# Product of gate and up kept in PSUM, unpaced sends, and earlier or split loads in an eight-layer hybrid kernel

## The reference

```python
x = x + attn_a(layernorm(x))        # layer 0, 16 heads of 8
x = x + experts(layernorm(x))       # layer 1
x = x + attn_b(layernorm(x))        # layer 2, 32 heads of 32
x = x + experts(layernorm(x))       # layer 3
x = x + attn_pos(layernorm(x))      # layer 4, bias from a FIR filter table
x = x + int8_ffn(layernorm(x))      # layer 5
x = x + linear_attention(layernorm(x))   # layer 6
x = x + int8_ffn(layernorm(x))      # layer 7

def experts(x):                     # 7 routed experts, top 2, DFF = 512
    out = swiglu(x, shared_gate, shared_up, shared_down)
    probs = softmax(x @ router_w.T)
    top_vals, top_idx = top_k(probs, 2)
    top_vals = top_vals / (top_vals.sum(-1) + 1e-9)
    for e in range(7):
        out += combine[:, e] * swiglu(x, gate[e], up[e], down[e])
    return out                      # swiglu: (silu(x @ gate.T) * (x @ up.T)) @ down.T
```

## Time and profile before

| what | value |
|---|---|
| time, median of three runs | 4055.63 us |
| profiled execution: its own time | 4050.18 us |
| profiled execution: span of the trace | 4048.4 us |
| PE busy (matmul) | 3387.4 us, 84% |
| DVE busy | 3025.4 us, 75% |
| ACT busy | 2472.5 us, 61% |
| POOL busy | 1173.4 us, 29% |
| layers 1 and 3 (experts) | about 812 to 1223 us and 2511 to 2923 us of the span |
| layers 5, 6, 7 | about 3551 to 3622, 3628 to 3961, 3968 to 4040 us |

### The profile page before, as it was taken

One profiled execution on the slowest core, in us unless ns is written; L12 is line 12 of the kernel. 1 busy time (PEld: TensorE's weight loads), 2 busy tenths in 40 slices (PEclk: granted clock), 3 DMA queues, 4 the chain that ended last, 5 costly groups with the idle time before them and its releaser, 6 DMA issues. The chain is left out here.

```text
span 4048.4 us, 57724 instructions
## 1 busy us (share of the span) xinstructions
PE 3387.4 (84%) x18344; PEld 2100.8 (52%) x18344; DVE 3025.4 (75%) x7013; ACT 2472.5 (61%) x4541; POOL 1173.4 (29%) x920
## 2 busy tenths in 40 slices
PE   5888888677964999999999997879499999858875
PEld 3555555465742455555455554657366666533433
DVE  6999999665874677777776773668778888659985
ACT  3888888534741556556555563457279999752325
POOL 1000000034431556665665664434300000010111
PEclk9999999878986999999999997889799999978887
DMA  4222221112435666767676660134332222200000
GB/s 130 46 53 53 46 37 24 29 49 91 145 106 86 87 88 85 89 83 89 82 90 84 88 87 9 51 113 140 100 106 47 46 30 47 34 26 0 0 0 27
DMA packets 218722, 265.93 MB, mean 66 GB/s; under 512 B 95745, under 2 KB 123714, under 8 KB 218295
## 3 DMA queue, kind: packets, MB, share of 16 engines
q1 hardware_dynamic: 208694, 241.25, 33.8%
q0 software_dynamic: 9728, 20.99, 1.5%
HBM read 103.36 MB, written 57.08 MB: 40 GB/s over the span
## 5 line engine op out<-in xcount | busy, mean ns | idle before, releaser
L1157 DVE TENSOR_REDUCE at_b_top<-ps 128x1 f32<-128x512 f32 x1024 | 662.5, 682 | 354.8 <-PE ps L917 353.5
L1046 ACT ACTIVATE at_b_e<-ps 128x512 f32<-128x512 f32 x1024 | 583.4, 598 | 474.7 <-PE ps L923 461.4
L585 ACT ACTIVATE at_a_e<-at_a_logits,at_a_neg_top 128x512 f32<-128x512 f32 x1024 | 655.9, 715 | 122.0 <-DVE at_a_neg_top L645 120.4
L816 POOL TENSOR_TENSOR at_b_e_pair<-at_b_e 128x1024 f32<-128x1024 f32 x256 | 603.1, 2376 | 403.1 <-PE ps L945 400.8
L505 PE MATMUL ps<-at_a_in_k,at_a_in_q 96*128 96x512 f32 x1024 | 477.9, 492 | 143.2 <-DVE at_a_clipped L613 116.9
L917 PE MATMUL ps<-at_b_k,at_b_q 96*128 96x512 f32 x1024 | 500.0, 492 | 41.0 <-DMA at_b_k<-at_b_k_hi 38.6
L923 PE MATMUL ps<-at_b_q,at_b_k 98*128 98x512 f32 x1024 | 426.9, 418 | 19.7 <-ACT at_b_e L1046 19.2
L641 DVE CUSTOM_DVE_ANT_0 at_a_logits<-ps,at_a_in_strip 128x512 f32<-128x512 f32 x512 | 340.7, 689 | 84.3 <-PE ps L505 33.7
L505 PEld LDWEIGHTS ps<-at_a_in_k,at_a_in_q 96*128 96x128 f32 x1024 | 185.0, 190 | 355.6 <-DVE at_a_clipped L613 206.6
L613 DVE TENSOR_SCALAR at_a_clipped<-ps 128x512 f32<-128x512 f32 x512 | 352.6, 689 | 21.3 <-PE ps L505 20.2
L635 DVE CUSTOM_DVE_ANT_0 at_a_logits<-at_a_clipped,at_a_in_decay_strip 128x512 f32<-128x512 f32 x512 | 347.6, 684 | 0.0
(11 more groups left out here) (334 smaller groups left out, 6451.4 us busy)
## 6 DMA issues: line engine op xcount, KB each, us to landing
moe_stage<-in_moe_w SPq DMA_DIRECT2D x46, 768.0 KB, 4.3
at_b_q<-at_b_q_hi SPq DMA_DIRECT2D x128, 256.0 KB, 5.4
at_b_k<-at_b_k_hi SPq DMA_DIRECT2D x128, 256.0 KB, 7.4
at_b_q<-at_b_q_lo SPq DMA_DIRECT2D x64, 256.0 KB, 7.6
at_b_k<-at_b_k_lo SPq DMA_DIRECT2D x64, 256.0 KB, 7.9
slot_rows<-empty_slots SPq DMA_DIRECT2D x44, 288.0 KB, 4.8
moe_xg<-slot_rows SPq DMA_DIRECT2D x44, 288.0 KB, 4.6
at_a_in_q<-q_hi SPq DMA_DIRECT2D x128, 64.0 KB
```

The source lines that it names most:

```text
L585: act.activation(e[:, j, qb, :], logits[:, j % 2, qb, :], ACT.Exp, bias=neg_top[:, j % 2, qb:qb + 1]).then_inc(exp_done, 1)
L816: pool.tensor_tensor(e_pair[:, j, :, :], e[r][:, j, 0:2, :], e[r][:, j, 2:4, :], ALU.add).then_inc(pair_done, 1)
L1046: act.activation(e[r][:, j, b, :], g.ps[:, ST_BANK + b % 2, :], ACT.Exp).then_inc(exp_done, 1)
L1157: dve.tensor_reduce(top[:, t, j, qb:qb + 1], g.ps[:, bank, :], AX_X, ALU.max).then_inc(max_done, 1)
```

## The change

It has four parts. None changes what is computed.

1. **h stays in PSUM.** The buffer `h` is gone. DVE writes `gate * up` back over the up bank (`h_bank`), and `high_h` and `low_h` read it there. The bank may be overwritten only when `low_h` has read it, so `gate_up(m)` now waits for `h_lo_done` of step m - 2 where it waited for `h_done` of step m - 2.
2. **Sends and row weights.** The waits that paced the sends are removed. The weights `c1`, `c2` are computed earlier (before the counts arrive from PE) and travel with the sent rows, in one more column of `xs`. A routed unit's rows are multiplied by their weight when they leave PSUM: four instructions of 128x128 (`tensor_scalar`) in place of one copy of 128x512. At the end of a turn PE adds the two rows of a token in PSUM with two identity matmuls for each batch, and DVE adds the sum to `x_all` with one instruction of 128x512. Rows are numbered so that a partition's rows lie together in DRAM, and the loads go round three buffers.
3. **Constants and weights.** The 13 loads of the linear attention's constants are issued in layer 5, POOL sets their zeros and ones there, and the buffers stay allocated through layer 6. The converted weights `w` of layer 5 are kept for layer 7, which no longer loads and converts them.
4. **The table in two pieces.** `table` is loaded as rows 0 to 95 and rows 96 to 100, ahead of `taps` and `wp`.

```diff
@@ begin, SP
                     if b == 1:
-                        for dst, src in ((taps, a["taps"]), (table, a["line_table"]), (wp, a["wpos"])):
+                        for rows in (slice(0, 96), slice(96, 101)):
+                            sp.dma_start(table[rows], a["line_table"][rows]).then_inc(table_loaded, 16)
+                        for dst, src in ((taps, a["taps"]), (wp, a["wpos"])):
                             sp.dma_start(dst[:], src).then_inc(table_loaded, 16)
...
+class LinearConstants:
...
+    def zero(self, pool):
+        pool.memset(self.from_m[:], 0.0).then_inc(self.zeroed, 1)
+        pool.memset(self.one_row[:], 1.0).then_inc(self.zeroed, 1)
+
+    def load(self, sp):
...
+            sp.dma_start(dst, src).then_inc(self.loaded, 16)
...
@@ linear_attention: SP's list of loads and DVE's memsets removed
@@ integer_swiglu, SP / ACT / POOL / DVE
-                sp.dma_start(stage[:], packed[0]).then_inc(w_loaded, 16)
+                if first:
+                    sp.dma_start(stage[:], packed[0]).then_inc(w_loaded, 16)
+                    ahead.load(sp)
+                    sp.wait_ge(ahead.loaded, 16 * ahead.LOADS)
...
-                act.wait_ge(w_float, 1)
-                act.activation(w[:], stage_f[:], ACT.Copy).then_inc(w_done, 1)
+                if first:
+                    act.wait_ge(w_float, 1)
+                    act.activation(w[:], stage_f[:], ACT.Copy).then_inc(w_done, 1)
...
+                if first:
+                    ahead.zero(pool)
...
@@ dispatch_experts, SP
-                for b in range(B):
-
-                    wait(sp, added, TB * (b - 1))
+                for b in range(1, B + 1):
+
+                    wait(sp, summed, b - Y_RING)
                     for k in range(2):
...
+                        rows = g.y_slots[k * B * S:(k + 1) * B * S, :].rearrange("(p t) d -> p t d", t=T)
+                        sp.dma_start(pair(b, k).rearrange("p (t d) -> p t d", t=TB), rows[:, (b - 1) * TB:b * TB, :]
+                                     ).then_inc(y_loaded[(b - 1) % Y_RING], 16)
@@ POOL
                 def send(k, half):
                     for t in range(half * HALF, (half + 1) * HALF):
-
-                        unit, place = divmod(k * T + t, SENT_PER_UNIT)
-                        if place == 0 and unit < B:
-                            pool.wait_ge(gate_done, nth(unit + 1, 0))
-                        elif place == 0 and unit == B:
-                            pool.wait_ge(h_lo_done, C * B)
                         pool.indirect_dma_start(slots, bass.IndirectOffsetOnAxis(ap=pos[k][:, t:t + 1], axis=0),
                                                 xs[:, t, :], None).then_inc(sent[2 * k + half], 16)
 
+                pool.wait_ge(c_done, 2)
                 pool.wait_ge(pos_done, 1)
@@ PE
                     wait(pe, gate_done, m - 2)
-                    wait(pe, h_done, m - 2)
+                    wait(pe, h_lo_done, m - 2)
...
+                pe.wait_ge(h_done, C * UNITS)
+                for b in range(1, B + 1):
+                    pe.wait_ge(y_loaded[(b - 1) % Y_RING], 32 * ((b - 1) // Y_RING + 1))
+
+                    wait(pe, added, b - 2)
+                    for k in range(2):
+                        ins = pe.matmul(g.ps[:, G_BANK + b % 2, :], g.ident[:], pair(b, k), start=(k == 0), stop=(k == 1))
+                    ins.then_inc(summed, 1)
@@ ACT and DVE
-                    act.activation(h_hi[:, (m - 1) % C, :], h[:, m % 2, :], ACT.Copy).then_inc(h_hi_done, 1)
+                    act.activation(h_hi[:, (m - 1) % C, :], h_bank(m), ACT.Copy).then_inc(h_hi_done, 1)
...
-                    dve.tensor_tensor(h_lo[:, (m - 1) % C, :], h[:, m % 2, :], h_hi[:, (m - 1) % C, :].bitcast(F32),
+                    dve.tensor_tensor(h_lo[:, (m - 1) % C, :], h_bank(m), h_hi[:, (m - 1) % C, :].bitcast(F32),
                                       ALU.subtract).then_inc(h_lo_done, 1)
...
-                        dve.tensor_copy(y_tok[u % 2][:], y).then_inc(out_taken, 1)
+                        dve.wait_ge(share_done, slot_of(u) + 1)
+                        for s in range(TB):
+                            ins = dve.tensor_scalar(y_tok[u % 2][:, s, :], y[:, s, :],
+                                                    share[:, slot_of(u) % 4, s:s + 1], None, ALU.mult)
+                            ins.then_inc(out_taken if s == TB - 1 else y_scaled, 1)
...
-                                dve.tensor_tensor(h[:, m % 2, :], gate[:, m % 2, :], g.ps[:, U_BANK + m % 2, :], ALU.mult
-                                                  ).then_inc(h_done, 1)
+                                dve.tensor_tensor(h_bank(m), gate[:, m % 2, :], h_bank(m), ALU.mult).then_inc(h_done, 1)
...
-                            dve.scalar_tensor_tensor(g.x_all[:, t, :], stage[:, (b - 1) % 2, tb * DM:(tb + 1) * DM],
-                                                     c1[:, t:t + 1], g.x_all[:, t, :], ALU.mult, ALU.add
-                                                     ).then_inc(first_added, 1)
...
+                        x = batch_of(g.x_all, b)
+                        dve.tensor_tensor(x, g.ps[:, G_BANK + b % 2, :].rearrange("p (t d) -> p t d", t=TB), x, ALU.add
+                                          ).then_inc(added, 1)
```

More of the change, by code:

```diff
@@ L1787, in integer_swiglu @@
     with Phase(nc, name) as ph:
-        stage = ph.sb("stage", [P, W], I32)
-        stage_f = ph.sb("stage_f", [P, W])
-        w = ph.sb("w", [P, W], F32R)
+        first = ahead is not None
+        stage = ph.sb("stage", [P, W], I32) if first else None
+        stage_f = ph.sb("stage_f", [P, W]) if first else None
         shift = ph.sb("shift", [P, TILES])
@@ L1870, in _ @@
                         pe.wait_ge(x_lo_done, s - 1)
-                        if s - 1 == 1:
+                        if first and s - 1 == 1:
                             pe.wait_ge(w_done, 1)
@@ L2044, in w_load, with pair @@
             return 0 if u <= B else slot_of(u) + 1
+        def pair(b, k=None):
+            both_rows = stage[:].rearrange("p a w -> p (a w)")[:, (b - 1) % Y_RING * 2 * S:((b - 1) % Y_RING + 1) * 2 * S]
+            return both_rows if k is None else both_rows[:, k * S:(k + 1) * S]
         def w_part(part):
```

144 lines of the change are left out of this document (71 added, 73 removed).

## The result

The changed kernel took **4403.93 us** (median of four runs, 4400.92 to 4407.03), the kernel before beside it 4055.14 us: ratio 1.086, 95% interval 1.0841 to 1.0879, 349 us slower. The forecast had the direction and the largest term, but with 4265 us it is 139 us short, and 4404 lies outside its range. The same kernel measured a second time (run e16, on chip 0; which chip the first measurement used is not recorded) took **4277.00 us** (4276.51 to 4277.61; before beside it 4048.62 us; ratio 1.0565, interval 1.0547 to 1.0582). Nearly the whole miss of 139 us is the difference of 127 us between these two measurements. I call their profiles "after, first" (span 4402.5 us) and "after, second" (4274.9 us).

A forecast was written before the change was run, and what follows sets the result against it. PE was taken to bound the routed units (busy 209.65 of 215 us). Terms 296 - 44 - 15 - 16 - 8 - 3 = +210 on the profiled 4050.18 gave 4260, 5 us under the median, so 4265 us; range 4215 to 4380.

The forecast's parts named there:

- h in PSUM: Expert layers' steps: gate_up's wait for h_lo closes a chain, 3.65 us a step, +296 us for both turns.
- rival 1: Expert units: PE's clock falls in the chain's pauses; 4.95 us a step, 4567 us at half clock; chance 0.10.
- Rival 2: Expert units: the chain doesn't close, steps keep 2.38 us; 3969 us; chance 0.06.
- Sends without a pace: Gap before the routed units: sends stay hidden, PE waits only for DVE's last output; -22 us a turn, -44.
- the cover is ample: Sends: 64 take 82 us, ending near 942, with shared units ending near 975, so even slower sends stay hidden.
- The bound from above: Sends without a pace: nothing is lost if POOL is slower, down to 1.8 us a send.
- Start: Kernel's start: split table spreads over the DMA engines, last batch at 12.5; -16 us, bounds 0 and -18.
- End of a turn: First load to last statistics: 21.3 us in place of 28.8; -15 for both turns, bounds +11 and -20.
- Layers 6 and 7: ACT starts layer 6 earlier, -8 us; layer 7's x_hi starts when the transposes end, -3 us; layer 5 stays.
- Output and weight arithmetic: Routed units' four-part output and earlier weight arithmetic: counted at nothing; output 20 us without cover.
- theories A, C and K: Follow-up theories of the stall: A, unpaced sends whatever the chain; C, only closed chains exposed; K, VectorE's PSUM writes.

The follow-up runs named there:

- e16: The changed kernel itself, unchanged, measured a second time on chip 0: 4277.00 us, ratio 1.057.
- e1: Changed kernel with the pace of six sends a shared unit back, h still in PSUM, chip 8: 4322.07 us, ratio 1.068.
- e4: Changed kernel with h back in an SBUF buffer of its own and the pace of six back, chip 8: 4012.59 us, ratio 0.991.
- e5: Changed kernel with the pace back and h_lo(m-1), h_hi(m-1) ahead of h(m), gate(m) in DVE's and ACT's lists, chip 8: 4017.95 us.
- e12: Changed kernel, unpaced, POOL waiting after every eight sends until they landed (acted in turn 1 only), chip 7: 4345.88 us, ratio 1.070.
- e15: Changed kernel with h in SBUF, no pace, and the table in one piece again, chip 6: 4124.06 us, ratio 1.016.
- e17: e3 unchanged, measured again on chip 0: 3979.45 us, ratio 0.983.
- e3: Changed kernel with h back in SBUF, sends without a pace, chip 8: 3976.02 us, ratio 0.982.
- e18: e4 unchanged, measured again on chip 0: 4009.24 us, ratio 0.990.

## Why the prediction was right and wrong

**h in PSUM: right.** Forecast +296, measured 309.5 (e1 against e4). The step was 3.72 us and not 3.65. Four of five links came out within 0.03 us; `h_lo` to PE was 0.83 and not 0.74. I had read that link at a `down` and it now ends at a `gate_up`; whether that is the reason no run shows. PE's clock stayed at 0.99, so rival 1 did not come (by the Trainium skill's TensorE: Matmul & The Clock Gate, A second HAM failure mode, it should have in part; the trace disagrees). Rival 2 would have needed the order of e5.

**Sends without a pace: the step that failed.** It said "the cover is ample", "nothing is lost if POOL is slower", and priced only how long POOL takes. Two halves came out differently. The gap did shrink as said, by 22.0 and 22.2 us a turn in after, second (-44), and by nearly as much in after, first (gaps of 13.1 and 12.4 us). But the step let the sends run beside the shared units at no cost to them, and in the first measurement they cost 178.6 - 113.8 = 64.8 us and 65.1 us, together 130 us: the term was some +86 there and not -44. Short stops hold this off, as e12 shows (117.3 us in the turn with them, 178.4 in the turn without). The pace had such stops, and the kernel before ran on chips 6 and 7 too, at 4056 and 4062 us. The changed kernel with the pace was not run there. The rows ahead of the prediction could not show the cost, since POOL stops there for a gate after at most twelve sends, and the last sixteen run when the shared units are over. The bound from above should have allowed that these stops were needed. What in the chip delays PE's completions stays open.

**Start: right.** Forecast -16; -14.9 by e15 against e17, -15.9 from the traces of before and after (814.7 and 798.8). The advice not to split a transfer, since the halves serialize (the Trainium skill, DMA: Bandwidth & Descriptors, Rules for kernel authors), doesn't carry over to these 101 rows: the DMA share from 3 to 8 us was 0.96 with the split (after, second) and 0.09 without it (e15). Whether the two pieces serialize no run shows. A small slip of mine: 2.2 MB at 290 GB/s is 7.6 us, not 7.9.

**End of a turn: too large.** Forecast -15, measured 5.3 us in the second turn, some -10 for both. The mis-sized term is PE's. The window 3144 to 3153 shows 15 matmuls in 6.65 us at full clock, 0.44 us each, and a batch has four of them (32 in all): 1.8 us, which I had only for half clock, and half of it later. DVE waits 0.25 to 0.86 us for PE in every batch from the third on.

**Layers 6 and 7: right in sum.** `lin_xn` starts 8.2 us earlier (-8). From layer 7's `shift` to the end it takes 76.8 us in place of 79.7 (-3). Two small ones I had at 0: layer 5 is 3 us shorter, and layer 6 itself 1.7 us longer.

**Output and weight arithmetic: nearly nothing.** With h in SBUF a routed step takes 2.405 us (e3, e4) in place of 2.384, 1.8 us a turn. I put it down to the four-part output, which no run takes out by itself.

Sum for after, second: the steps (113.8 - 72.2) + (320.3 - 205.0) = 156.9 us a turn, 320.3 from the gate of step 34 to that of step 120. 314 (steps) - 44 - 16 - 10 - 8 - 3 - 3 + 2 = 232 us, against 226.5 between the spans. The forecast had 210. With the 130 us of lateness the 226.5 become 356, against the first measurement's 354 between spans. That 4265 lies only 12 us from the second measurement is in part luck: against the kernel before beside it the change cost 228 us there, and that kernel was itself some 6 us faster than the 4055 from which I had started.

## What to carry to other kernels

A wait that only moves forward in one engine's list can close a loop through the lists of the others: follow it once round, with the order of every list, before pricing it at its length; here the cure that keeps h in PSUM was to swap two instructions in the lists (e5, 4018 us); moving h back (e4, 4013 us) cures it as well. A pace on a stream of indirect DMAs is not idle time until something else has been shown to fill it: e3 is the fastest kernel (ratio 0.982) where nothing gets late, but e15, which differs only in the table, was 1.6% slower than before where something does, while the kernel before, with its pace, kept its time on all chips. The kernel to choose is by this e4, h in SBUF with the pace (0.991, and 0.990 as e18), though it was not run on chips 6 and 7. A control belongs on the chip of the run that it controls: theories A, C and K each looked proved here by a comparison across chips. And whether an edit acts is read from the trace in every turn: e12's pause stood in the code of both and in the execution of one.

## What the runs showed of the hardware

- While POOL issues 1.26 us indirect DMAs of 128 rows back to back, PE's completions can reach ACT about 20 us late (20.16 in after, first). In after, first, e15 and the second turn of e12 the first late gate was due 11 to 15 us (nine to twelve sends) after the first send, and the last one came 8 to 9 us after the last send. A stop of 1.3 us or more after every eight sends held it off (e12, turn 1). POOL itself is not slowed (1.26 us a send in both). ACT to DVE and DVE to PE keep their 0.63 and 0.83 us. SP is late as well (two issues 4.91 us and not 0.89).
- All six unpaced kernels on chips 6 and 7 were late, whatever operation was added, and with an open or a closed chain, and so was the unpaced turn of e12; the six unpaced runs on chips 8 and 0 were not. Each chip was seen on one occasion, chip 8 on two, so whether it is the chip or its state at the time is open; so is what holds PE's completions up. Not tried: the kernel before without a pace, e3, e4 and the changed kernel with the pace on chips 6 and 7, and smaller indirect DMAs.
- VectorE and ScalarE take the same time on h in PSUM as in SBUF: h 0.70 and 0.69 us, `h_hi` 0.59 and 0.62, `h_lo` 0.68 and 0.68.
